# Folding an expert sum on the way back: four plain transposes and two adds in place of four products with a folding matrix

## The reference, cut to what matters

```python
def _L0_ffn_ref(x, gate_w, gate_b, w1, b1, w2, b2, gamma, beta):     # E, K = 16, 2
    gate_logits = x @ gate_w + gate_b
    topk_vals, topk_idx = jax.lax.top_k(gate_logits, K)
    topk_w = jax.nn.softmax(topk_vals, axis=-1)
    h = jax.nn.relu(jnp.einsum('bsh,ehf->bsef', x, w1) + b1)
    expert_out = jnp.einsum('bsef,efh->bseh', h, w2) + b2
    sel = jnp.take_along_axis(expert_out, topk_idx[:, :, :, None], axis=2)
    moe = jnp.sum(topk_w[..., None] * sel, axis=2)
    y = x + moe
    ...                                   # layernorm of y over its 64 values, times gamma, plus beta
```

## Time and profile before

| | |
|---|---|
| median of 3 runs | 739.51 us (738.17 to 740.5) |
| the profiled execution's own time | 737.55 us |
| its span in the trace | 735.8 us |
| mean granted TensorE clock | 0.983 of full speed |
| TensorE busy | 645.7 us, 88% |
| VectorE busy | 570.9 us, 78% |
| ScalarE busy | 502.1 us, 68% |
| GpSimd busy | 334.1 us, 45% |

### The profile page before, as it was taken

The page is one execution under the profiler, slowest core; times in us unless marked ns, Lnnn a source line. Parts: engine busy times, 40 slices in busy tenths (PEclk is TensorE's granted clock), DMA queues, the critical chain, the costliest instruction groups (busy, mean ns, idle before and its releaser), DMA issues. The chain is left out here.

```text
span 735.8 us, 16590 instructions
## 1 busy us (share of the span) xinstructions
PE 645.7 (88%) x5070; PEld 353.0 (48%) x5070; DVE 570.9 (78%) x1647; ACT 502.1 (68%) x1264; POOL 334.1 (45%) x417
## 2 busy tenths in 40 slices
PE   4557998999999988899999988799888988888896
PEld 4524655666666653233332224455555655553332
DVE  6677787777777775899999989779988888867653
ACT  2747877888888872677777767658777777745542
POOL 1007678688787885223232334725445644320000
PEclk9869999999999999999999999999999999999998
DMA  4030000000000001633233330000000000000011
GB/s 111 1 114 1 2 2 0 0 0 0 0 0 0 1 1 47 204 100 108 96 116 115 110 109 16 2 2 1 1 0 0 0 0 0 2 1 2 15 22 22
DMA packets 22038, 24.37 MB, mean 33 GB/s; under 512 B 12390, under 2 KB 12902, under 8 KB 21734
## 3 DMA queue, kind: packets, MB, share of 16 engines
q1 hardware_dynamic: 19751, 23.31, 10.5%
q10 hardware_dynamic: 2239, 0.49, 0.3%
HBM read 22.48 MB, written 1.31 MB: 32 GB/s over the span
## 5 line engine op out<-in xcount | busy, mean ns | idle before, releaser
L1358 POOL TENSOR_TENSOR big<-big 128x1024 f32<-128x1024 f32 x64 | 119.8, 1893 | 44.2 <-DVE big L1172 44.2
L956 ACT ACTIVATE big<-ps,big 128x255 f32<-128x255 f32 x256 | 117.0, 483 | 10.0 <-DVE big L1166 7.5
L918 ACT ACTIVATE big<-ps,b1s 128x512 f32<-128x512 f32 x128 | 80.1, 678 | 31.1 <-PE ps L650 30.0
L1166 DVE TENSOR_REDUCE big<-ps 128x4 f32<-128x1020 f32 x64 | 75.1, 1212 | 25.0 <-PE ps L726 25.0
L1962 ACT ACTIVATE big<-ps 128x1024 f32<-128x1024 f32 x64 | 65.9, 1030 | 33.1 <-PE ps L1589 30.7
L2104 DVE TENSOR_REDUCE big<-ps 128x4 f32<-128x1020 f32 x64 | 78.0, 1219 | 6.9 <-DVE res L2161 2.5
L732 PE MATMUL ps<-cst,big 128*128 128x128 f32 x512 | 76.7, 283 | 6.3 <-POOL big L1358 2.4
L1178 DVE COPY mid<-ps 128x512 f32<-128x512 f32 x96 | 63.4, 685 | 18.3 <-PE ps L732 15.1
L732 PEld LDWEIGHTS ps<-cst,big 128*128 128x128 f32 x512 | 54.2, 140 | 40.8 <-issue 21.5
L650 PE MATMUL ps<-big,wall 64*128 64x512 f32 x256 | 72.1, 640 | 0.7 <-ACT big L889 0.7
L661 PE MATMUL ps<-big,w2s 128*64 128x512 f32 x256 | 69.0, 617 | 3.1 <-ACT big L918 1.8
(11 more groups left out here) (276 smaller groups left out, 1329.9 us busy)
## 6 DMA issues: line engine op xcount, KB each, us to landing
mid<-spread_w SPq DMA_DIRECT2D x128, 128.0 KB, 2.8
mid<-in_split_sel SPq DMA_DIRECT2D x1, 1536.0 KB, 7.0
wall<-in_w SPq DMA_DIRECT2D x1, 1280.0 KB, 6.1
out_tokens<-res SPq DMA_DIRECT2D x16, 56.0 KB, 1.6
cst<-in_consts SPq DMA_DIRECT2D x1, 520.5 KB, 4.9
pexp<-in_w_raw SPq DMA_DIRECT2D x1, 512.0 KB, 6.5
w2s<-in_w SPq DMA_DIRECT2D x1, 512.0 KB, 3.4
mid<-in_taps ACTq DMA_DIRECT2D x1, 320.0 KB, 3.9
```

The source lines that it names most:

```text
L918: last = nc.scalar.activation(hid[e % 2][j], H1(e, j), ACT.Relu, bias=b1s[0][:, 2 * e + j:2 * e + j + 1])
L956: last = nc.scalar.activation(e_sb[r % 4][:, jj, tq, 0:NW], S[:, 2 * (r % 2) + jj, tq, 0:NW], ACT.Exp, scale=-1.0, bias=minus[r % 4][:, jj ...
L1166: nc.vector.tensor_reduce(minus[r % 4], S[:, 2 * a:2 * a + 2, :, 0:NW], AX.X, ALU.min).then_inc(s_mx, 1)
L1358: nc.gpsimd.tensor_tensor(e_sb[r % 4], e_sb[r % 4], bc(inverse[r % 4].unsqueeze(3), [P, 2, 2, 256]), ALU.mult).then_inc(s_A, 1)
```

## The change

`sum_turn` no longer multiplies by `fold`. It transposes each block of 128 x 128 of `acc` against the identity, so that the two halves stand beside each other in R: for tile t the columns 128t to 128t+63 are the even experts' half, 128t+64 to 128t+127 the odd experts'. R is now written over all its 512 columns. `total` adds the first halves to `x2` into `yy`, waits on a new semaphore of VectorE's own, and adds the second halves to `yy` in place. `s_tot` is raised by the second add.

```diff
@@ tower / attention0_and_experts0
+            s_part_tot = sem("e0_first_half_added")
@@ sum_turn
                     for k in range(TC):
-                        last = nc.tensor.matmul(R[:, D * k:D * k + D], acc[q][:, P * k:P * k + P], fold[:], start=True, stop=True)
+                        last = nc.tensor.transpose(R[:, P * k:P * k + P], acc[q][:, P * k:P * k + P], ident)
                     last.then_inc(s_yt, 1)
@@ finish
                     def total():
+                        halves = R.rearrange("p (t j d) -> p t j d", t=TC, j=2)
                         dve.wait_ge(s_yt, c + 1)
-                        nc.vector.tensor_tensor(yy, R[:, 0:TC * D].rearrange("p (t d) -> p t d", t=TC), x2[:, tl, 0], ALU.add).then_inc(s_tot, 1)
+                        nc.vector.tensor_tensor(yy, halves[:, :, 0], x2[:, tl, 0], ALU.add).then_inc(s_part_tot, 1)
+                        dve.wait_ge(s_part_tot, c + 1)
+                        nc.vector.tensor_tensor(yy, halves[:, :, 1], yy, ALU.add).then_inc(s_tot, 1)
                         dve.wait_ge(s_tot, c + 1)
```

## The result

Twenty runs of each kernel: 740.66 us before, 736.04 after, ratio 0.9946 with a 95% interval of 0.9924 to 0.9968, so 2.4 to 5.6 us less. It is faster, as forecast; the forecast of 2.66 us less (ratio 0.9964) lies inside the interval, near its end. A second measurement of the same kernel gave 0.9965 (0.9942 to 0.9988), that is 2.6 us.

The account below looks back on a forecast made before the run. The bound was taken to be a chain passing between TensorE and VectorE through the sum turn. Seven turns at -0.42 us (-2.94) and +0.28 at the eighth gave -2.66, from 739.51 to 736.9 us, range 734.8 to 739.8.

Parts of the forecast that it names:

- What bounds: In a middle chunk of 20.37 us: sum turn 1.01, `hidden(3)` and `second(2)`, then 16.7 us of VectorE until the next turn.
- 1.07 us "issue": VectorE's idle time before L1152 of duo 2 in each of seven chunks, read as waiting for `second(2)`; 7.5 us in all.
- the rival of something that does not move: VectorE's wait before L1152 is for, say, a weight buffer; chunks stay as they are, 739.8 us; chance 0.08.
- The turn: Sum turn on TensorE: four transposes take 0.59 instead of 1.01 us to the next `hidden`, saving 0.42 in each of seven chunks.
- The second add: In `total` on VectorE: 0.46 us with its wait, hidden in the seven chunks with 0.15 to spare.
- The rival of a costlier add: Second add on VectorE outlasts its cover: 737.9 us, chance 0.10; or so long that the kernel is slower, 742.6, chance 0.04.
- The eighth turn: In the preparation of the second attention, without cover for the second add: `stats` comes 0.28 us later, all counted as lost.
- The rival that the end gives more: Preparation of the second attention: shifted engines avoid one or two slow adds beside GpSimd, about -3.5 to -4, 735.7 us; chance 0.07.
- The sum: Whole kernel: -2.94 us from seven turns plus 0.28 from the eighth, -2.66 in all; chance 0.68.
- The clock: TensorE's clock stays 1.00 in the chunks; rival: transposes don't hold it, +5.9 us, 745.4, chance 0.03.
- one sign of being wrong: TensorE's clock in the windows falling under 1.00 was named beforehand as showing the prediction wrong.

Follow-up runs that it names:

- turn_only: The changed kernel without the second add, so the odd experts' half is left out of the sum; ratio 0.996 to the kernel before.
- second_add_only: The kernel before, still multiplying by `fold`, with the add of `total` done twice; ratio 0.9989 to the kernel before, 1.0006 in a second look of one round.
- third_add: The changed kernel with its first add done twice, so three adds; ratio 0.9974 to the kernel before.
- after_again: The changed kernel measured again with no edit; ratio 0.9965 to the kernel before.
- after_selectors_later: The changed kernel with the 1.5 MB transfer of the second layer's selectors moved behind the weight rows of chunk 1; ratio 0.9944 to the kernel before.
- last_by_fold: The changed kernel with only the eighth turn done by the product with `fold` and one add; ratio 0.9928 to the kernel before.
- later_turn_fold: The kernel before, with `fold` and one add, but the sum turn issued one duo later, after `second(2)`; median 730.52 us, ratio 0.9862 to the kernel before.
- later_turn_transposes: The changed kernel with its sum turn issued one duo later, after `second(2)`; ratio 0.9916 to the kernel before.

## Why the prediction was right

- *What bounds.* The chain sum turn, `hidden(3)`, `second(2)`, then VectorE without a gap to L1041, held in every kernel: turn_only, second_add_only and third_add give middle chunks of 19.92, 20.37 and 20.23, each to about 0.01 of what it says. That the 1.07 us "issue" was a wait for `second(2)` was an inference from times; it shrank by just what TensorE came earlier and VectorE worked longer (1.07, 0.64, 0.61, 0.18, none), so the rival of something that does not move falls.
- *The turn.* 0.59 taken from L615, 0.56 to 0.59 measured; 0.42 a chunk forecast; 0.44 to 0.46 measured in six distances between turns and 0.18 in the first, in all 2.87 for a forecast of 2.94. That the first came out short goes mostly with a weight transfer that VectorE waited for, and the sum had no term for that.
- *The second add.* 0.46 forecast, 0.45 measured, and hidden with 0.18 idle, 0.15 forecast. The rival of a costlier add falls by L1096's 0.425 as its longest. What such a price would do, third_add shows.
- *The eighth turn.* +0.28 forecast, +0.28 measured, handed on whole. This is the smallest term and the only one against the gain. The rival that the end gives more has a number (735.7) nearer to the median of 736.04 than the forecast's, but what it rests on did not come: from the first L453 behind the eighth turn to the end of the trace it is 280.48 us before and 280.76 in after_again.
- *The sum.* -2.66 forecast; the stretch gave -2.59, the two measurements -4.0 (2.4 to 5.6) and -2.6. No step failed. That the median of 736.04 lies only 0.9 us under the forecast is in part luck: the forecast started from three runs with a median of 739.51, and twenty gave 740.66. By the medians the kernel gained 4.6 us where 2.7 were forecast, and only the second measurement and the stretch say that 2.6 is the size of it.
- *The clock.* The windows of the middle chunks stay at 1.00, that is 2.4 GHz, with twelve transposes in a chunk in place of eight. The rule of the Trainium skill (TensorE: Matmul & The Clock Gate, Part 4, PE-mode transpose), that the full clock does not engage for transposes, does not show here: four more of them among 64 longer passes neither lowered nor raised it. By the letter one sign of being wrong did come, a window under 1.00, in chunk 1 of the first profile. But the same falls came in second_add_only, which turns by `fold`, so they don't speak for this rival. Its price was also too high. The 550 ns of the earlier trace rows is the first pass of that line alone, in a place where the window shows no lower clock (its neighbours took 421), so it is not a price of the lower clock. In the first profile of the changed kernel four fp32 transposes ran while the granted clock was low (0.50 in the window from 648 to 650, shown above) and took 0.99 to the next product, 0.40 more than the earlier trace rows, not 1.10:

```profile
649.50 1.06 PE L1615 MATMUL ps<-cst,big 128*128 128x128 f32 x4
...
650.49 0.61 PE L1593 MATMUL ps<-big 64*128 64x256 bf16 x4
```

- *What was not seen.* The prediction took the order of the work as given. The same rows, 1.18 us idle on TensorE and 1.07 on VectorE in each middle chunk, said that an order in which neither waits would be worth 7.5 us; it measured 7.7 in the stretch. The ratio's interval is 8.7 to 11.7; the part above 7.7 is not explained by the chain.

## What to carry to other kernels

When two engines hand a chain back and forth, each idle a little in every round, price an edit by where it stands on the chain and by how much cover its other half has: here 0.42 us counted seven times and 0.46 us once. Then look at the two idle times themselves: moving the hand-over one step later was worth three times the edit, and it turned the sign of the edit. A trade of one engine's time for another's has no price of its own, only one in a given order.

## What was not expected of the hardware

TensorE's clock sometimes falls to its lower level, 1.2 GHz, after it has stood idle before a sum turn. In the first profile of the changed kernel it was idle 2.30 us before the turn of chunk 1, and the windows behind show a granted clock of 0.62 and 0.53; chunk 1 was 20.77 long instead of 19.72. In the first profile of second_add_only it was idle 1.34 and 1.44 before the turns of chunks 1 and 7, and both times fell behind them:

```profile
314.00:316.00 2.00, 2.00 (x6) 0.29 (x4) 1.03 (x5) 0.59 (x2) 0.00 (x0) 0.50 0.71 201
...
438.00:440.00 2.00, 2.00 (x6) 0.29 (x4) 0.23 (x2) 1.28 (x3) 0.00 (x0) 0.52 0.31 114
```

The four passes of a `hidden` then took 2.08 us instead of 1.13:

```profile
436.60 2.08 PE L651 MATMUL ps<-big,wall 64*128 64x512 f32 x4
```

Other executions had the same waits and kept 1.00 (1.59 and 1.44 in the kernel before, 2.40 in after_selectors_later), so the wait alone does not decide it. Falls also come in the second layer, far from any sum turn: one between 640 and 700 us in most of these traces, two in the first profile of the changed kernel and in turn_only, none in last_by_fold.

The times of single runs go with the clock: 732.40 us at a mean clock of 0.986, 742.81 at 0.971, both of the changed kernel. Over the 81 runs of the kernel before that were taken beside the experiments, a mean clock higher by 0.01 goes with about 5.7 us less (correlation -0.82). That bears on the ratios that came out lower than the stretch says, by 2.0 us in third_add, 2.2 in last_by_fold and 2.5 in both kernels with the later order. Last_by_fold and third_add keep the wait before the turn, so its absence in the later order is not what made the difference. The mean clocks of these four kernels were 0.982 to 0.984, against 0.979 and 0.980 in the runs of the kernel before beside them. An estimate, the difference of the means with 5.7 us for each 0.01 of clock taken out, against what the stretch gave: after_again -2.8 (-2.6), turn_only -2.8 (-3.1), third_add -0.4 (+0.1), last_by_fold -3.0 (-3.1), later_turn_fold -8.7 (-7.7), later_turn_transposes -4.9 (-3.7). So most of the excess goes with the clock, except about 1 us in the later order. Why one set of runs had fewer falls than another was not tested.
